# Second normalisation computed inside layer 0's last loop for six of eight tiles

## The reference

```python
def _layernorm(x, axis=-1, eps=1e-05):
    m = jnp.mean(x, axis=axis, keepdims=True)
    v = jnp.var(x, axis=axis, keepdims=True)
    return (x - m) / jnp.sqrt(v + eps)
...
    # layer 0 attention: 32 query heads of 16, one key and value head, ALiBi bias, causal
    q = (hidden_states @ Wq).reshape(b, s, NUM_HEADS, HEAD_DIM)
    kv = hidden_states @ Wkv
...
    # layer 0 feed-forward: weights looked up by 4-bit codes, 8-bit ones for tokens with a norm over 64
    e = jnp.linalg.norm(x, axis=-1) * LIN_SLOPE + LIN_INTER
    mask = e > EST_T
...
    y = jnp.where(mask[..., None], y_h, y_l) + bias
...
    x = L0_attn_hidden_states                      # (1, 1024, 512), float32
    xn = _layernorm(x, axis=-1)
    x = x + _L0_attn_ref(xn, ...) + _L0_ffn_ref(xn, ...)
    xn = _layernorm(x, axis=-1)                    # the second normalisation
    x = x + _L1_attn_ref(xn, ...) + _L1_ffn_ref(xn, ...)
    return x
```

## Time and profile before

| | |
|---|---|
| median of 3 runs | 1765.18 us (1763.39 to 1767.66) |
| the profiled execution's own time | 1769.56 us |
| its span, first to last instruction | 1767.8 us |
| mean granted TensorE clock | 0.981 |
| TensorE busy | 93% of the span, 10959 matmuls and transposes |
| VectorE, ScalarE, GpSimd busy | 63%, 40%, 46% |
| HBM traffic over the span | 22 GB/s |

### The profile page before, as it was taken

One profiled execution on the slowest core, in us unless ns is written; L12 is line 12 of the kernel. 1 busy time (PEld: TensorE's weight loads), 2 busy tenths in 40 slices (PEclk: granted clock), 3 DMA queues, 4 the chain that ended last, 5 costly groups with the idle time before them and its releaser, 6 DMA issues. The chain is left out here.

```text
span 1767.8 us, 32007 instructions
## 1 busy us (share of the span) xinstructions
PE 1646.9 (93%) x10959; PEld 1273.1 (72%) x10959; DVE 1112.4 (63%) x1898; ACT 709.1 (40%) x1483; POOL 819.2 (46%) x808
## 2 busy tenths in 40 slices
PE   5788999997889999999999999999999999979999
PEld 4444444456778878878878878878878878867887
DVE  6877788324866766676676676676576576544333
ACT  4435556751155145145245235335325325432221
POOL 4087999400643553553453453364354354134331
PEclk9989999999999999999999999999999999989999
DMA  6440000001110000000000010001001001012101
GB/s 128 55 67 3 2 2 2 3 14 35 41 31 13 19 25 19 19 25 19 19 25 19 13 31 19 13 20 30 8 18 36 1 18 55 1 48 66 42 14 48
DMA packets 36054, 47.05 MB, mean 27 GB/s; under 512 B 11757, under 2 KB 18125, under 8 KB 35901
## 3 DMA queue, kind: packets, MB, share of 16 engines
q1 hardware_dynamic: 35922, 45.11, 10.5%
HBM read 37.56 MB, written 2.10 MB: 22 GB/s over the span
## 5 line engine op out<-in xcount | busy, mean ns | idle before, releaser
L1566 DVE TENSOR_TENSOR ptnl<-ps,ptnh 128x512 fp32r<-128x512 f32 (+1 forms) x320 | 204.0, 638 | 136.2 <-ACT ptnh L1484 130.2
L1484 ACT ACTIVATE ptnh<-ps 128x512 fp32r<-128x512 f32 (+1 forms) x320 | 177.8, 556 | 268.6 <-PE ps L1410 265.9
L71 PE MATMUL ps<-xth,wh 128*128 128x512 f32 (+1 forms) x560 | 225.6, 403 | 5.7 <-POOL wl L2027 4.1
L73 PE MATMUL ps<-xth,wl 128*128 128x512 f32 (+1 forms) x560 | 222.8, 398 | 0.0
L72 PE MATMUL ps<-xtl,wh 128*128 128x512 f32 (+1 forms) x560 | 222.7, 398 | 0.0
L1554 DVE TENSOR_REDUCE negm<-ps 128x1 f32<-128x768 f32 (+3 forms) x224 | 183.5, 819 | 34.6 <-PE ps L1388 32.0
L71 PE MATMUL ps<-ptnh,vh 128*128 128x256 f32 x576 | 183.7, 319 | 10.7 <-DVE ptnl L1566 10.2
L1656 POOL TENSOR_SCALAR pshort<-pshort,rinv 128x128 f32<-128x128 f32 (+3 forms) x64 | 34.4, 537 | 277.0 <-DVE rinv L1591 277.0
L73 PE MATMUL ps<-ptnh,vl 128*128 128x256 f32 x576 | 161.3, 280 | 0.0
L72 PE MATMUL ps<-ptnl,vh 128*128 128x256 f32 x576 | 160.7, 279 | 0.0
L718 ACT ACTIVATE pt<-ps 128x512 f32<-128x512 f32 x226 | 131.4, 596 | 70.8 <-PE ps L509 45.2
(11 more groups left out here) (225 smaller groups left out, 3870.0 us busy)
## 6 DMA issues: line engine op xcount, KB each, us to landing
raw<-in_w SPq DMA_DIRECT2D x48, 256.0 KB, 2.6
raw<-in_wo SPq DMA_DIRECT2D x32, 256.0 KB, 2.6
qstack<-qpart SPq DMA_DIRECT2D x40, 128.0 KB, 5.3
raw<-in_gate_main SPq DMA_DIRECT2D x10, 256.0 KB, 2.7
raw<-in_up_main SPq DMA_DIRECT2D x10, 256.0 KB, 2.8
raw<-in_down_main SPq DMA_DIRECT2D x10, 256.0 KB, 2.6
resid<-in_x SPq DMA_DIRECT2D x4, 512.0 KB, 5.4
out<-resid SPq DMA_DIRECT2D x8, 256.0 KB, 2.0
```

What stands on the lines that cost most here:

```text
L71: pe.matmul(out, lh, rh, start=first, stop=False)
L73: return pe.matmul(out, ll, rh, start=False, stop=last)
L1484: nc.scalar.activation(ptnh[:, i % PT_RING, 0:w], ps[:, b, 0:w], ACT.Copy).then_inc(high_ready, 1)
L1566: nc.vector.tensor_tensor(ptnl[:, i % PT_RING, 0:w], ps[:, b, 0:w], ptnh[:, i % PT_RING, 0:w].bitcast(F32), ALU.subtract).then_inc(low_rea ...
```

## The change

Layer 0's last loop now also does the second normalisation of tiles 0 to 5, in pairs. When the adds of an odd tile t < 6 are done, VectorE aggregates the statistics of tiles t - 1 and t, ScalarE takes their root, and VectorE refines it and writes two tiles `nxn` (`next_pair`). At t = 3, 5 and 7 TensorE transposes the pair t - 3, t - 2 (`turn_next`), behind the transposes of the attention output. ScalarE copies the high parts one turn later, and VectorE subtracts for the low parts at even t (`next_lows`). VectorE makes `attl` of the next tile straight behind the adds, and takes the statistics of the same tile after it. The flag is read ahead of the loop on TensorE and VectorE. The parts go to `xth` and `xtl`, which are kept for layer 1; layer 0 has others of its own (`xth0`, `xtl0`), and other buffers are laid over each other to make room.

SP loads layer 1's first three weight chunks in layer 0, with the 8-bit table behind the first of them, and GpSimd splits them there. In layer 1 `Norm` handles tiles 6 and 7 alone, the constants are loaded first, and chunk 3 is the first weight load. Some semaphores are merged (in the gated part too). The branch that is skipped grows by the same normalisation for its own case.

```diff
@@ -82,13 +84,28 @@
 
         keep = {
             "resid": sb("resid", [P, ST, D], F32),
-            "xth": sb("xth", [P, DT, S], F32R),
-            "xtl": sb("xtl", [P, DT, S], F32R),
             "identf": sb("identf", [P, P], F32),
             "identb": sb("identb", [P, P], BF16),
             "masku": sb("masku", [P, P], BF16),
             "stats": sb("stats", [P, ST, 6], F32),
         }
+        def overlaid(**shapes):
+
+            with ExitStack() as early:
+                for name, (shape, dt) in shapes.items():
+                    keep[name] = early.enter_context(nc.sbuf_tensor(name, shape, dt))
+
+        overlaid(qstack=([P, H0, S], BF16))
+        keep["xth"], keep["xtl"] = sb("xth", [P, DT, S], F32R), sb("xtl", [P, DT, S], F32R)
+        overlaid(hidh=([P, HSLOTS, S], F32R), hidl=([P, HSLOTS, S], F32R))
+        keep["wh"], keep["wl"] = sb("wh", [P, W_RING, BLK], F32R), sb("wl1", [P, W_RING, BLK], F32R)
+        keep["wraw"] = sb("wraw", [P, RAW_RING, BLK], F32)
+        overlaid(luth=([P, DT, CODES_H], F32), nxn=([P, 2, D], F32))
+        keep["kth"], keep["ktl"] = sb("kth", [P, S], F32R), sb("ktl", [P, S], F32R)
+        keep["vh"], keep["vl"] = sb("vh", [P, ST, P], F32R), sb("vl", [P, ST, P], F32R)
+        keep["raw_in"] = [ctx.enter_context(nc.semaphore(f"raw_in{i}")) for i in range(RAW_RING)]
+        keep["w_high"], keep["w_split"] = ctx.enter_context(nc.semaphore("w_high")), ctx.enter_context(nc.semaphore("w_split"))
+        keep["waited"] = ctx.enter_context(nc.semaphore("waited"))
         layer0(nc, a, keep)
 
...
 
+def refine(nc, dve, step, r, sd, t, veps):
+
+    n = step.inc(nc.vector.reciprocal(r, sd))
+    dve.wait_ge(step.sem, n)
+    n = step.inc(nc.vector.tensor_tensor(t, r, r, ALU.mult))
+    dve.wait_ge(step.sem, n)
+    n = step.inc(nc.vector.tensor_tensor(t, t, veps, ALU.mult))
+    dve.wait_ge(step.sem, n)
+    n = step.inc(nc.vector.tensor_scalar(t, t, -0.5, 1.5, ALU.mult, ALU.add))
+    dve.wait_ge(step.sem, n)
+    n = step.inc(nc.vector.tensor_tensor(r, r, t, ALU.mult))
+    dve.wait_ge(step.sem, n)
+
...
             atth, attl = sbl("atth", [P, 2, DT, P], F32R), sbl("attl", [P, 2, DT, P], F32R)
-        luth = qstack[:, 0:2, :].rearrange("p h s -> p (h s)").bitcast(F32).rearrange("p (c k) -> p c k", c=DT)
+        wnh, wnl, wraw, luth, nxn = (keep[n] for n in ("wh", "wl", "wraw", "luth", "nxn"))
+        nxth, nxtl = keep["xth"], keep["xtl"]
+        nmv = sb("nmv", [P, ST, 2])
+        nveps, nsd, nr, nt = (sb(n, [P, ST]) for n in ("nveps", "nsd", "nr", "nt"))
         with ExitStack() as rare:
...
             sp.wait_ge(head_done, HG0 * ST + 1)
-            sp.dma_start(luth, a["lut8"].rearrange("(c p) k -> p c k", p=P)).then_inc(luth_in, 16)
+            for c in range(W_RING):
+                if c >= RAW_RING:
+                    sp.wait_ge(keep["w_split"], c - RAW_RING + 1)
+                sp.dma_start(wraw[:, c % RAW_RING, :], a["w1"][0, c]).then_inc(keep["raw_in"][c % RAW_RING], 16)
+                if c == 0:
+                    sp.dma_start(luth[:], a["lut8"].rearrange("(c p) k -> p c k", p=P)).then_inc(luth_in, 16)
             sp.wait_ge(luth_in, 16)
 
 
...
                 last.then_inc(att_turned, 1)
 
+            def turn_next(s):
+
+                pe.wait_ge(next_ready, s + 1)
+                if s >= 2:
+                    pe.wait_ge(next_low, s - 1)
+                for c in range(DT):
+                    last = nc.tensor.transpose(ps[:, s % 2, c * P:(c + 1) * P], nxn[:, s % 2, c * P:(c + 1) * P], identf[:])
+                last.then_inc(next_turned, 1)
+
             turn_att(0)
             pe.wait_ge(flag_ready, 1)
+            some = pe.value_load(flag[0:1, 0:1], min_val=0, max_val=1)
             for t in range(ST):
                 if t >= 2:
                     pe.wait_ge(x1_ready, t - 1)
...
                     turn_att(t + 1)
+                if t % 2 and t >= 3:
+                    turn_next(t - 3)
+                    turn_next(t - 2)
                 pe.wait_ge(att_low, t + 1)
                 pe.wait_ge(wo_low, DT)
...
                 last.then_inc(o_ps, 1)
 
-
-            some = pe.value_load(flag[0:1, 0:1], min_val=0, max_val=1)
             with pe.If(some > 0):
                 pe.wait_ge(rare_w, 1)
...
                 nc.scalar.activation(wlh[:, c, :], bank(c), ACT.Copy).then_inc(wl_high, 1)
-            for t in range(ST):
+            for t in range(ST + 1):
+                if t and t % 2 and t >= 3:
+                    pair = slice(t - 3, t - 1)
+                    act.wait_ge(next_veps, t // 2)
+                    nc.scalar.activation(nsd[:, pair], nveps[:, pair], ACT.Sqrt).then_inc(next_sd, 1)
+                if t % 2 == 0 and t >= 4:
+                    for s in (t - 4, t - 3):
+                        act.wait_ge(next_turned, s + 1)
+                        nc.scalar.activation(nxth[:, :, s * P:(s + 1) * P], ps[:, s % 2, :].rearrange("p (c s) -> p c s", c=DT),
+                                             ACT.Copy).then_inc(next_high, 1)
+                if t == ST:
+                    break
                 act.wait_ge(att_turned, t + 1)
                 if t >= 2:
                     act.wait_ge(o_ps, t - 1)
...
             nc.vector.tensor_reduce(flag[:], ps[0:1, 4, 0:P], AX.X, ALU.max).then_inc(flag_ready, 1)
 
+            dve.wait_ge(flag_ready, 1)
+            some = dve.value_load(flag[0:1, 0:1], min_val=0, max_val=1)
             dve.wait_ge(wl_turned, 1)
             for c in range(DT):
                 dve.wait_ge(wl_high, c + 1)
...
 
-            for t in range(ST):
+            next_count = Count(norm_step)
+            next_count.n = HG0 * ST
+
+            def next_pair(t):
+
+                pair = slice(t - 1, t + 1)
+                dve.wait_ge(norm_step, next_count.n)
+                for s in (t - 1, t):
+                    n = next_count.inc(nc.vector.bn_aggr(nmv[:, s, :], keep["stats"][:, s, :]))
+                dve.wait_ge(norm_step, n)
+                nc.vector.tensor_scalar(nveps[:, pair], nmv[:, pair, 1], EPS, None, ALU.add).then_inc(next_veps, 1)
+                dve.wait_ge(next_sd, t // 2 + 1)
+                refine(nc, dve, next_count, nr[:, pair], nsd[:, pair], nt[:, pair], nveps[:, pair])
+                for s in (t - 1, t):
+                    if s >= 2:
+                        dve.wait_ge(next_turned, s - 1)
+                    nc.vector.tensor_scalar(nxn[:, s % 2, :], resid[:, s, :], nmv[:, s, 0:1], nr[:, s:s + 1],
+                                            ALU.subtract, ALU.mult).then_inc(next_ready, 1)
+
+            def next_lows(s):
+                dve.wait_ge(next_turned, s + 1)
+                dve.wait_ge(next_high, s + 1)
+                nc.vector.tensor_tensor(nxtl[:, :, s * P:(s + 1) * P], ps[:, s % 2, :].rearrange("p (c s) -> p c s", c=DT),
+                                        nxth[:, :, s * P:(s + 1) * P].bitcast(F32), ALU.subtract).then_inc(next_low, 1)
+
+            def att_part(t):
                 dve.wait_ge(att_turned, t + 1)
                 dve.wait_ge(att_high, t + 1)
                 if t >= 2:
                     dve.wait_ge(o_ps, t - 1)
                 nc.vector.tensor_tensor(attl[:, t % 2, :, :], bank(6 + t % 2).rearrange("p (c s) -> p c s", c=DT),
                                         atth[:, t % 2, :, :].bitcast(F32), ALU.subtract).then_inc(att_low, 1)
+
+            att_part(0)
+            for t in range(ST):
                 dve.wait_ge(o_ps, t + 1)
                 nc.vector.tensor_tensor(xn[:, t, :], ps[:, 2 + t % 2, :], resid[:, t, :], ALU.add).then_inc(t_ready, 1)
                 dve.wait_ge(t_ready, t + 1)
                 dve.wait_ge(y_ps, t + 1)
                 nc.vector.tensor_tensor(resid[:, t, :], ps[:, 4 + t % 2, :], xn[:, t, :], ALU.add).then_inc(x1_ready, 1)
-                if t:
-                    next_stats(t - 1)
-            next_stats(ST - 1)
-
-
-            some = dve.value_load(flag[0:1, 0:1], min_val=0, max_val=1)
+                if t + 1 < ST:
+                    att_part(t + 1)
+                dve.wait_ge(x1_ready, t + 1)
+                next_count.inc(nc.vector.bn_stats(keep["stats"][:, t, :], resid[:, t, :]))
+                if t % 2 and t < EARLY:
+                    next_pair(t)
+                if t % 2 == 0 and t >= 2:
+                    next_lows(t - 2)
+                    next_lows(t - 1)
+
             with dve.If(some > 0):
                 step = Count(rare_step)
...
             codes(EARLY_CODES, CODES_L)
+            for c in range(W_RING):
+                pool.wait_ge(keep["raw_in"][c % RAW_RING], 16 * (c // RAW_RING + 1))
+                pool.sem_inc(waited, 1)
+                nc.gpsimd.tensor_scalar(wnh[:, c, :], wraw[:, c % RAW_RING, :], 1.0, 1.0, ALU.mult, ALU.mult).then_inc(keep["w_high"], 1)
+                pool.wait_ge(keep["w_high"], c + 1)
```

(35 more changed lines are left out.)

## The result

The changed kernel took 1778.59 us (median of 4 runs, 1777.99 to 1781.99) where the kernel before took 1766.42 us beside it: a ratio of 1.0076, 95% interval 1.0058 to 1.0094. The forecast was 1757.7 us and "faster". The profiled execution took 1781.99 us, with a span of 1779.8.

The account below looks back on a forecast made before the run. TensorE bounds the kernel, so gains lie in its idle stretch before P1: +2.15 (transposes) - 0.50 (tail) - 1.22 (seam) - 7.98 (block to P1) = -7.55 us, so 1765.2 becomes 1757.7 us, range 1754.6 to 1761.5.

Parts of the forecast that it names:

- Part 6: Stretch behind P1: constants and chunk 3 come in time, nothing new is late, so the 7.5 us reach the end.
- P1: Moment layer 1's second projection fill starts, the forecast's measure: 450.79 us before, 443.25 forecast, 7.5 us earlier.
- the gain isn't passed on: Rival: constants, chunk 3 or the larger skipped block come late behind P1; gain 0 to 3 us, 1762 to 1765; chance 0.12.
- The rival that forecast a slower kernel: VectorE becomes the bound of layer 0's last loop, TensorE stops for attl; about 1769 us; chance 0.03.
- Part 1: Layer 0's last loop: 24 more transposes on a full TensorE cost +2.15 us, bounds +1.8 to +2.6.
- Part 2: VectorE in layer 0's last loop: the pair's normalisation ends at T + 5.4, before the next o(t); cost nothing.
- T: Moment in a turn of layer 0's last loop at which VectorE sees o(t); the next is seen at T + 5.9.
- Part 3: Seam between layer 0 and layer 1's block: flag read moved to the start shortens it from 3.12 to 1.9 us.
- Part 4: VectorE's tail of layer 0: one statistics instruction instead of two behind the last add, 2.60 to 2.10 us.
- Part 5: Layer 1's start: first fill at block + 0.95, lasting 4.1 us, then 2.7 us to P1, at 443.25.
- first rival: Full seam, clock cold throughout: block at 436.7, fill up to 5.1 us, P1 at 445.5, 1759.9 us; chance 0.20.
- high clock: Rival: clock stays high with a short seam, first fill 2.8 us, P1 at 441.7, 1756.1 us; chance 0.10.

Follow-up runs that it names:

- 64 clears: Changed kernel plus 64 never-executed VectorE memsets in the skipped branch, so its group loop is well placed: 1759.55 us, ratio 0.9970.
- 32 clears: Changed kernel plus 32 never-executed VectorE memsets in the skipped branch: ratio 0.9965.
- short branch: Changed kernel with VectorE's skipped branch as a machine loop instead of eight written-out copies, 155 instructions instead of 378: 1761.1 us, ratio 0.9948.

## Why the prediction was wrong, step by step

**The step that failed is Part 6**, "behind P1 nothing new is late, and the 7.5 us should reach the end". It looked for late loads and splits, and TensorE indeed has no gap in the stretch behind P1; but it put code that isn't edited at no cost, without a reason. VectorE's jump back went from 0.24 to 2.7 us, six times. Against the well placed version that is 11.3 us of waits and 8.3 us of a lower clock; against the kernel before, the six turns last 19.7 us longer. The rival "the gain isn't passed on" named a second fetch of 2.1 us, but once, at the skipped branch, not in every turn of a loop; it ended within "no change" and had 0.12. The rival that forecast a slower kernel (0.03) blamed VectorE in layer 0's loop, where TensorE never waits; it had the direction by another mechanism.

With that term taken out (64 clears), the forecast's own sum can be read. It gave -7.5 us; the ratios with 64 and 32 clears are 0.9970 and 0.9965, which is -5.3 and -6.2 us.

**Part 1** (+2.15, bounds 1.8 to 2.6): from VectorE's last jump ahead of the loop to the last o product it is 70.07 us in the kernel before (429.34 less 359.27) and 72.46 in the changed one (431.43 less 358.97): +2.4. Right, a little low. **Part 2** (nothing, pair done at T + 5.4): T is 393.50 and the second nxn write ends at 398.86, T + 5.36. Right.

**Part 3** (seam 3.12 -> 1.9 us): 2.45 us, the term that was mis-sized here. I had taken 0.95 us of the seam for the flag's read. In the kernel before:

```profile
L1011 DVEq TENSOR_LOAD <-flag x1: 546/546/546, 430.8 to 430.8; - x1
L1012 DVEq COMPARE_BRANCH  x1: 56/56/56, 431.7 to 431.7; - x1
```

The read ends at 431.35 and the branch stands at 431.72, 0.45 us behind the start of the last statistics (431.27 to 431.95); in the changed kernel it follows that start by 0.01 us. So the read cost 0.43 us of the seam, and most of it lay under the statistics. The 0.95 us belong to the jump: its fetch starts 1.15 us behind the branch in the kernel before (432.93), 0.95 in the changed one (433.90), and 0.92 to 0.94 behind each jump back of the changed kernel's loop. The other 0.24 us that were won are a shorter jump, 2.76 us from its end to VectorE's next instruction against 3.0; it is 2.75 to 3.01 in all runs with the long branch, and no run shows what sets it. The short branch shows that the rest is the fetch of the target. The Trainium skill ("Runtime: NRT & Kernel Launch", Instruction fetch mechanics) says that a taken branch whose target is outside the window of prefetched pages waits for a DMA of that page. The traces agree, by 2.7 us and more with a fetch in the jump and 0.5 us without one, and a loop's jump back turns out to be such a branch too. I had cited the rule for one jump and not asked it of the others. The same section of the Trainium skill gives blocks of 16 KiB, of which two are held in most engines. VectorE's fetches here are of 8 KB, which decides it for this case, and its loop of 300 instructions (19 KB) is held when it is well placed.

**Part 4** (2.10): 431.43 to 433.57, 2.14. Right.

**Part 5** (first fill at block + 0.95, half-clock fill of 4.1 us, then 2.7): 0.91, 4.63 and 2.69. The fill ran at the low level from its start, with 0.43 us between matmuls up to 440.5, so the fill is 0.5 us over my value and within the 4.4 to 4.7 us that its rows gave; I had gone below them for a reason that didn't hold. P1 is 444.25 (forecast 443.25), 6.5 us earlier than before instead of 7.5. That lies between the forecast and its first rival (P1 at 445.5). The rivals of a high clock and of a VectorE bound in the loop didn't happen.

The books close: at the second write of k0h the changed kernel is 6.7 us ahead, in the next six turns it loses 19.7, and from there to the end it is 1.0 us shorter. Sum +12.0 us, the difference of the two spans; the ratio of 1.0076 is +13.4 us.

## What to carry to other kernels

Code that you don't touch has a price that depends on where it lies: when an edit lengthens an engine's program ahead of a loop that is not unrolled, compare that loop's jump back (end of the branch to the first instruction at its head) and the number of instruction fetches on the profile's page, before and after, before you explain anything else. If a change is slower for no reason in its own stretch, run it once with never-executed instructions in a branch that is skipped: it costs one run and separates what the change does from where it puts the rest. A rule about jumps must be asked of every jump of the program, the ones in loops first, as they are paid in every turn.

## What the runs showed of the hardware that was not expected

- VectorE's loop of 300 instructions jumps back in 0.22 to 0.27 us at starts with a remainder by 128 of 77 to 115 or 3, and in 2.7 to 2.9 us at 45 to 53, with five fetches of 8 KB per turn instead of none. Six jumps cost 18 to 22 us in all, more than their own length, since the clock falls behind some of the gaps: matmuls of 0.28 us take 0.42.
- TensorE's jump back of 3.7 us with nine 16 KB fetches per turn cost nothing here (0.9998 without it), as its sequencer reached it 4.3 us before VectorE.
- The jump over a skipped branch takes VectorE 2.75 to 3.01 us with 340 to 506 instructions skipped and 0.5 us with 155, and it overlaps the engine's last instruction. The fetch of its target starts 0.94 to 1.19 us behind it. A read of the flag from memory (0.55 us) ran under the statistics and held up the branch by 0.43 us.
